# A gated cross-attention and quantised feed-forward block: masks kept as bytes, added as 32-bit words, and a new order of instructions

## What is computed

```
scores = (ctx Wq^T + bq)(ctx Wk^T + bk)^T * H^-0.5 * layernorm(x)
scores = where(attn_mask | padding_mask, -inf, scores)
x = x + tanh(g0) * softmax(scores)
y = layernorm(x)
gate, up = silu(qlinear(y, w_gate)), qlinear(y, w_up)      # I = 2048
x = x + tanh(g1) * qlinear(gate * up, w_down)
```

## Time and profile before

| | |
|---|---|
| median of 3 runs | 228.04 us |
| the profiled execution | 227.88 us |
| its span on the core | 226.1 us |
| TensorE (PE) busy | 201.0 us, 89% |
| VectorE (DVE) busy | 175.3 us, 78% |
| ScalarE (ACT) busy | 131.5 us, 58% |
| GpSimd (POOL) busy | 127.7 us, 56% |

### The profile page before, as it was taken

One profiled execution on the slowest core, in us unless ns is written; L12 is line 12 of the kernel. 1 busy time (PEld: TensorE's weight loads), 2 busy tenths in 40 slices (PEclk: granted clock), 3 DMA queues, 4 the chain that ended last, 5 costly groups with the idle time before them and its releaser, 6 DMA issues.

```text
span 226.1 us, 2874 instructions
## 1 busy us (share of the span) xinstructions
PE 201.0 (89%) x854; PEld 90.8 (40%) x854; DVE 175.3 (78%) x343; ACT 131.5 (58%) x173; POOL 127.7 (56%) x180
## 2 busy tenths in 40 slices
PE   8714526979999998999999999999999999999994
PEld 7201104234444443444444444444444444444441
DVE  0588897899879899699969889897998675786221
ACT  2559986965989410466994305977655525771400
POOL 2898799999999998225168775117994000000000
PEclk9985555799999999999999999999999999999999
DMA  6999979865004466204235632414846626001982
GB/s 222 422 420 417 417 282 372 311 188 226 0 0 93 96 139 117 70 0 96 46 77 108 139 96 72 89 27 94 112 76 117 162 49 139 3 0 20 202 198 93
DMA packets 47360, 32.84 MB, mean 145 GB/s; under 512 B 40944, under 2 KB 41072, under 8 KB 45808
## 3 DMA queue, kind: packets, MB, share of 16 engines
q1 hardware_dynamic: 47200, 32.51, 50.9%
q10 hardware_dynamic: 144, 0.13, 0.3%
HBM read 18.48 MB, written 4.19 MB: 100 GB/s over the span
## 4 chain that ended last, share of the span: by engine, by line
PE 59%; POOL 23%; issue 7%; DVE 4%; DMA 4%; ACT 1%; SPq 0%; POOLq 0%; DVEq 0%
PE pD L978 20%; PE pU L962 19%; PE pG L949 18%; POOL down_w L548 3%; POOL mask_bias L467 2%; POOL up_w L548 2%; PE pA L926 2%; POOL x L504 2%; DMA hid<-in_masks 2%; POOL probs L517 2%; DVE x L1265 2%; POOL gate_w L548 2%; POOL probs L501 2%; DMA xqT<-xq 1%; POOL esd L512 1%
## 5 line engine op out<-in xcount | busy, mean ns | idle before, releaser
L747 ACT ACTIVATE hid<-pG,act_g 128x512 f32<-128x512 f32 x64 | 43.7, 686 | 52.9 <-PE pG L949 52.3
L949 PE MATMUL pG<-gate_w,xqT 128*128 128x512 f16 x256 | 65.0, 387 | 1.7 <-DMA xqT<-xq 1.0
L962 PE MATMUL pU<-up_w,xqT 128*128 128x512 f16 x256 | 62.1, 379 | 1.1 <-DVE up_w L1355 1.1
L978 PE MATMUL pD<-down_w,stage_b 128*128 128x512 f16 x256 | 57.9, 379 | 0.2 <-DMA stage_b<-stage_b 0.2
L1312 DVE TENSOR_TENSOR hid<-pU,hid 128x512 f32<-128x512 f32 x64 | 43.7, 685 | 13.3 <-PE pU L962 11.7
L754 ACT ACTIVATE stage_b<-hid,inv 128x1024 f16<-128x1024 f32 x32 | 35.7, 1141 | 16.1 <-DVE inv L1330 10.4
L949 PEld LDWEIGHTS pG<-gate_w,xqT 128*128 128x128 f16 x256 | 25.2, 99 | 38.0 <-issue 8.9
L962 PEld LDWEIGHTS pU<-up_w,xqT 128*128 128x128 f16 x256 | 24.9, 98 | 31.3 <-DVE up_w L1355 1.2
L978 PEld LDWEIGHTS pD<-down_w,stage_b 128*128 128x128 f16 x256 | 25.0, 98 | 30.6 <-issue 0.6
L555 POOL TENSOR_SCALAR out_scale<-den,act_e,down_k 128x1 f32<-128x1 f32 x16 | 5.4, 339 | 42.2 <-DVE den L1327 42.2
L467 POOL TENSOR_TENSOR mask_bias<-attn_bias,pad_bias 128x512 bf16<-128x512 bf16 x16 | 18.8, 1178 | 8.0 <-DVE mx L1249 7.8
(11 more groups left out here) (86 smaller groups left out, 232.1 us busy)
## 6 DMA issues: line engine op xcount, KB each, us to landing
stage_a<-in_L_ffn_w_gate SPq DMA_DIRECT2D x4, 1024.0 KB, 10.8
stage_b<-in_L_ffn_w_up SPq DMA_DIRECT2D x4, 1024.0 KB, 19.3
stage_a<-in_L_ffn_w_down SPq DMA_DIRECT2D x4, 1024.0 KB, 6.1
stage_b<-in_x SPq DMA_DIRECT2D x2, 1024.0 KB, 6.0
out<-x SPq DMA_DIRECT2D x8, 256.0 KB, 2.5
out<-stage_b SPq DMA_DIRECT2D x8, 256.0 KB, 2.4
ctx_s<-in_ctx SPq DMA_DIRECT2D x4, 256.0 KB, 5.7
x<-in_x SPq DMA_DIRECT2D x2, 512.0 KB, 7.8
```

The lines of the kernel that those rows point to most:

```text
L747: act.activation(hid[:, t % NH, n * 512:(n + 1) * 512], pG[c % NG][:, :], ACT.Silu, scale=act_g[:, t:t + 1]).then_inc(silu_done, 1)
L949: ins = pe.matmul(pG[c % NG][:, :], xqT[:, t // TILES % 2, t % TILES, k, :], gate_w[:, n, k, :], start=k == 0, stop=k == KD - 1)
L962: ins = pe.matmul(pU[c % NU][:, :], xqT[:, t // TILES % 2, t % TILES, k, :], up_w[:, n, k, :], start=k == 0, stop=k == KD - 1)
L978: ins = pe.matmul(pD[t % ND][:, :], hidT[:, t % 2, k, :], down_w[:, k // KD, k % KD, :], start=k == 0, stop=k == KI - 1)
```

## The change

The widenings are gone. The masks stay bytes (0 or 1); GpSimd reads them as 32-bit integers and adds the padding words of a batch to the attention words of all four tiles in one instruction, so a byte becomes 0, 1 or 2. mask_and_max subtracts the bytes from the scores and multiplies by 2^30; scores are scaled by 2^-80 ahead of it, and rstd is scaled back. q, k and ctx get four buffers instead of two, the bytes a buffer of their own.

```diff
-MASKED = -1.5e35
+SMALL = 2.0 ** -80
+BACK = 2.0 ** 30
+V1 = (SMALL * BACK) ** 2
+MASKED = -0.5 * BACK
 NEG = -3.4028234663852886e38
 SCALING = float(H) ** -0.5
...
 bqs = sb("bqs", [P, 1])
-ctx_s = sb("ctx_s", [P, 2, S])
-qT = sb("qT", [P, 2, S])
-kT = sb("kT", [P, 2, S])
-attn_bias = sb("attn_bias", [P, TILES, S], BF16)
-pad_bias = sb("pad_bias", [P, B, S], BF16)
-mask_bias = sb("mask_bias", [P, 2, S], BF16)
+ctx_s = sb("ctx_s", [P, NQ, S])
+qT = sb("qT", [P, NQ, S])
+kT = sb("kT", [P, NQ, S])
+masks_u8 = sb("masks_u8", [P, (TILES + B) * S], U8)
+mask_u8 = sb("mask_u8", [P, 2, TILES * S], U8)
 x01 = sb("x01", [P, 2 * TILES, D])
-probs = sb("probs", [P, TILES, S])
...
 def _(pool):
-    def pad_mask_bias(b0, b1):
-        pool.wait_ge(mask_loaded, 16)
-        pool.tensor_scalar(pad_bias[:, b0:b1, :], pad_u8[:, b0 * S:b1 * S].rearrange("p (b t) -> p b t", t=S),
-                           MASKED, 1.0, ALU.mult, ALU.mult).then_inc(bias_made, 1)
-    def attn_mask_bias(j0, j1):
-        pool.tensor_scalar(attn_bias[:, j0:j1, :], attn_u8[:, j0 * S:j1 * S].rearrange("p (j t) -> p j t", t=S),
-                           MASKED, 1.0, ALU.mult, ALU.mult).then_inc(bias_made, 1)
-    def mask(t):
-        b, j = divmod(t, TILES)
-        pool.wait_ge(bias_made, 2 if t == 0 else 3 if t < TILES else 4)
-        if t >= 2:
-            pool.wait_ge(masked, t - 1)
-        pool.tensor_tensor(mask_bias[:, t % 2, :], attn_bias[:, j, :], pad_bias[:, b, :], ALU.add)\
-            .then_inc(mask_ready, 1)
+    def mask(b):
+        if b == 0:
+            pool.wait_ge(mask_loaded, 16)
+        if b >= 2:
+            pool.wait_ge(masked, TILES * (b - 1))
+        w = S // 4
+        pad = masks_i32[:, (TILES + b) * w:(TILES + b + 1) * w].rearrange("p (j w) -> p j w", j=1)
+        pool.tensor_tensor(mask_i32[b % 2].rearrange("p (j w) -> p j w", w=w),
+                           masks_i32[:, 0:TILES * w].rearrange("p (j w) -> p j w", w=w),
+                           pad.broadcast_to([P, TILES, w]), ALU.add).then_inc(mask_ready, 1)
     def rstd(g):
...
         pool.wait_ge(masked, t1)
-        pool.tensor_scalar(valid[:, t0:t1], mx[:, t0:t1], MASKED / 2, 1.0, ALU.is_gt, ALU.mult)\
+        pool.tensor_scalar(valid[:, t0:t1], mx[:, t0:t1], MASKED, 1.0, ALU.is_gt, ALU.mult)\
             .then_inc(valid_done, 1)
         pool.wait_ge(valid_done, g + 1)
...
         if b == 0:
             act.wait_ge(bqs_done, 1)
-        if b >= 2:
-            act.wait_ge(score_done, TILES * (b - 1))
-        act.activation(qT[:, b % 2, :], pA[:, :], ACT.Identity, scale=SCALING, bias=bqs[:, :])\
+        if b >= NQ:
+            act.wait_ge(score_done, TILES * (b - NQ + 1))
+        act.activation(qT[:, b % NQ, :], pA[:, :], ACT.Identity, scale=SCALING * SMALL, bias=bqs[:, :])\
             .then_inc(q_ready, 1)
...
-        if t >= TILES:
-            quantised_x(dve, t - TILES)
-        dve.scalar_tensor_tensor(probs[:, t % TILES, :], xt(t), mv1[:, t, 0:1], bank[:, :],
+        if t >= NP:
+            quantised_x(dve, t - NP)
+        dve.scalar_tensor_tensor(probs[:, t % NP, :], xt(t), mv1[:, t, 0:1], bank[:, :],
                                  ALU.subtract, ALU.mult).then_inc(scored, 1)
     def mask_and_max(t):
         dve.wait_ge(scored, t + 1)
-        dve.wait_ge(mask_ready, t + 1)
-        dve.tensor_tensor_reduce(probs[:, t % TILES, :], probs[:, t % TILES, :], mask_bias[:, t % 2, :],
-                                 1.0, NEG, ALU.add, ALU.max, mx[:, t:t + 1]).then_inc(masked, 1)
+        b, j = divmod(t, TILES)
+        dve.wait_ge(mask_ready, b + 1)
+        dve.tensor_tensor_reduce(probs[:, t % NP, :], probs[:, t % NP, :], mask_u8[:, b % 2, j * S:(j + 1) * S],
+                                 BACK, NEG, ALU.subtract, ALU.max, mx[:, t:t + 1]).then_inc(masked, 1)
     def gate_sums(g):
```

More of the change, by code:

```diff
@@ L26 @@
 NH = 4
+NQ, NP = 2, 4
 NG, NU, ND = 2, 3, 2
@@ L586, in _ @@
             weight_round(0, 1)
+            weight_round(0, 2)
+            centre(2)
+            std2(1)
+            centre(3)
             gate_scales(0)
-            weight_round(0, 2)
-            std2(1)
-            centre(2)
             weight_round(0, 3)
-            centre(3)
-            mask(6)
             up_scales(0)
             weight_round(1, 0)
+            gate_scales(1)
+            quantise_x(2)
+            up_scales(1)
+            quantise_x(3)
             rstd(2)
             weight_round(1, 1)
-            mask(7)
@@ L599, in _ @@
-            quantise_x(2)
-            gate_scales(1)
-            quantise_x(3)
-            up_scales(1)
             weight_round(1, 2)
-            mask(8)
             weight_round(1, 3)
+            weight_round(2, 0)
             exp_bias(2)
-            weight_round(2, 0)
-            mask(9)
+            mask(3)
             weight_round(2, 1)
             weight_round(2, 2)
+            weight_round(2, 3)
             valid_sums(2)
-            weight_round(2, 3)
+            residual1(4)
@@ L1092, in _ @@
             up(6, 0)
-            gate(7, 0)
+            up(6, 1)
+            down(3, 0)
+            up(6, 2)
+            up(6, 3)
+            down(3, 1)
             down(3, 2)
-            up(6, 1)
             down(3, 3)
@@ L1386, in _ @@
             weight_bound(0, 1)
             stats2(3)
+            weight_bound(0, 2)
+            absmax_x(2)
             stats1(4)
-            weight_bound(0, 2)
+            inverse_std2(1)
             score(4)
-            stats1(5)
+            absmax_x(3)
             mask_and_max(4)
             copy_xT(0)
+            weight_scale(1)
             weight_bound(0, 3)
-            weight_scale(1)
-            inverse_std2(1)
+            reciprocal_scale(0)
+            inverse_x(1)
+            stats1(5)
@@ L1397, in _ @@
             stats1(6)
-            reciprocal_scale(0)
+            weight_bound(1, 0)
             stats1(7)
+            reciprocal_scale(1)
             score(5)
-            weight_bound(1, 0)
+            product(0, 0)
             mask_and_max(5)
-            absmax_x(2)
-            absmax_x(3)
-            product(0, 0)
-            inverse_x(1)
+            copy_xT(1)
+            product(1, 0)
+            weight_scale(2)
+            score(6)
             weight_bound(1, 1)
-            product(1, 0)
@@ L1409, in _ @@
-            score(6)
-            product(0, 1)
             mask_and_max(6)
             score(7)
-            absmax_hidden(0, 0)
-            mask_and_max(7)
-            weight_bound(1, 2)
-            product(1, 1)
-            weight_scale(2)
-            weight_bound(1, 3)
-            product(0, 2)
-            reciprocal_scale(1)
+            weight_bound(1, 2)
+            mask_and_max(7)
+            weight_bound(1, 3)
+            stats1(8)
+            product(0, 1)
+            stats1(9)
@@ L1431, in _ @@
             inverse_hidden(0)
+            product(1, 3)
+            stats1(10)
+            absmax_hidden(1, 1)
+            stats2(4)
+            inverse_hidden(1)
             product(2, 0)
-            absmax_hidden(1, 1)
-            weight_bound(2, 3)
+            stats2(5)
+            absmax_x(4)
             product(2, 1)
-            inverse_hidden(1)
-            absmax_hidden(2, 0)
+            stats1(11)
             product(2, 2)
-            stats2(4)
+            absmax_x(5)
+            stats2(6)
@@ L1440, in _ @@
+            inverse_std2(2)
             product(2, 3)
-            stats2(5)
-            absmax_hidden(2, 1)
-            stats2(6)
-            inverse_hidden(2)
+            inverse_x(2)
+            product(3, 0)
             residual2(0)
+            absmax_x(6)
+            score(8)
+            product(3, 1)
+            mask_and_max(8)
             stats2(7)
-            absmax_x(4)
-            inverse_std2(2)
-            stats1(8)
-            absmax_x(5)
-            product(3, 0)
@@ L1452, in _ @@
-            inverse_x(2)
-            inverse_std2(3)
-            absmax_x(6)
+            product(3, 2)
             residual2(1)
             absmax_x(7)
-            score(8)
-            inverse_x(3)
-            mask_and_max(8)
-            reciprocal_scale(2)
-            product(3, 1)
-            residual2(2)
+            score(9)
+            inverse_std2(3)
+            mask_and_max(9)
+            product(3, 3)
+            reciprocal_scale(2)
+            product(4, 0)
+            inverse_x(3)
```

630 lines of the change are left out of this document (304 added, 326 removed).

## The result

The changed kernel takes 231.53 us (median of 4 runs, 231.44 to 231.78), the kernel before 228.0 beside it (227.93 to 228.21, 4 runs): a ratio of 1.0147, 95% interval 1.0129 to 1.0165. It is 3.5 us slower; 229.7 was forecast, in a range of 225.2 to 232.0. One thing was said wrongly ahead: q, k and ctx keep their two buffers (`NQ, NP = 2, 4` in the kernel).

The account below looks back on a forecast made before the run. Bound by an opening of some 49 us, GpSimd and VectorE preparing TensorE's work, then TensorE's fixed list. List end 223.4 against 222.86 (+0.54) plus 1.3 of stalls gave +1.8 us: 229.7 us, range 225.2 to 232.0.

Parts of the forecast that it names:

- the opening's gain: Before the first weight rounding: 0.95 us won, turned into a loss of 1.8 us by the end of copy_xT(0).
- Mask arithmetic: GpSimd's masks and widenings: four integer adds of 1.25 us replace them, 18 to 19 us less work; byte operand free.
- To the first rounding: Opening: x's second part arrives at 13.4 us, first weight rounding starts near 24.7 us, gain 0.95 us.
- To the first gate: Roundings against VectorE instructions up to copy_xT(0): it ends at 39.1 us, before at 37.33.
- the tie: mask_and_max(4) against rounding 4 near 37 us: copy_xT(0) ends at 38.35 if it wins, 39.9 if it loses.
- of two VectorE instructions in a row the second keeps the way: Opening: a waiting rounding lets two successive VectorE instructions through; read from residual1 and weight_bound in the earlier trace.
- Rival 3: GpSimd gets its turn after every VectorE instruction; copy_xT(0) ends 1.1 us later, 231.6 us in all; chance 0.12.
- From the copy to score(6): copy_xT(0) to score(6): 11.2 us, including 2.2 for mask_and_max(5) against rounding (1, 1); score(6) starts at 50.3.
- The stalls: TensorE waits at up(1, 2) and up(2, 1) for products behind clips: 1.3 us taken, ends 0 and 2.5.
- The work behind: TensorE's list from score(6) on: 173.1 us of work, ending at 223.4 instead of 222.86 before stalls.
- the wait before gate(4, 0): TensorE's old wait of 0.95 us at 88.90 should go, as residual1(4) to quantise_x(4) shortens to about 12 us.
- Rival 1: Roundings and VectorE instructions pass each other; copy_xT(0) ends by 36.2 and the kernel takes 224.6 us; chance 0.27.

Follow-up runs that it names:

- the old order: New mask arithmetic with all five instruction lists in the order of the kernel before, one mask(b) replacing four mask(t), widenings left out: 225.23 us, 0.9874 against the kernel before.

## Why the prediction was right, and where it was off

The sign, the place and the mechanism were right: the opening's gain was lost to VectorE instructions that stand opposite roundings, and waits for products follow behind it. The size was 1.8 us too small, half of what was measured, and it would have been further off had a mask-and-max not got ahead of its rounding by luck (point 4).

1. **Mask arithmetic.** 1.25 us taken for the integer add, 1.27 measured. GpSimd's busy time fell by 19.8 us, 18 to 19 forecast. The two buffers of q, k and ctx change nothing in the sum, since four had been taken at zero. The byte operand costs nothing: an undisturbed mask-and-max takes 0.68 us, the mean is 0.80 (0.823 in the earlier trace rows).
2. **To the first rounding.** x's second part ended the wait as forecast (VectorE's stats start at 13.25, 13.4 forecast), and the rounding started at 24.39 (24.7). The halved clock of the earlier trace rows was misread: its slices stand at half from some 17 us on, not from 23; no term hangs on it. The add opposite residual1(0) costs here, 0.5 us, which the sum had left out; the run with doubled adds and the one with mask(1) in front both show it.
3. **To the first gate.** Forecast copy_xT(0) ended at 39.1, or 39.9 with the tie lost; it lost, at 40.05. But the way there wasn't mine. I had the second residual go straight through and the inverse at 30.5; it came at 31.9. This is the step that failed, "of two VectorE instructions in a row the second keeps the way": true of the earlier trace rows, where the second is a clip with constants, and false for two residuals. Rival 3 had this pair right, and the first clip waiting for rounding 3 (29.79, 1.86 us), with the copy ending at 40.2. Most of the 1.4 us was taken back by luck, at the other side of the same meeting: the roundings, held up by one instruction at a time instead of two, ended at 31.1 instead of 32.3, and the second clip, which I had waiting for the third of them, met nothing. mask_and_max(4) came at 37.47, 0.4 late.
4. **From the copy to score(6).** 11.2 us forecast, 9.25 measured (40.05 to 49.30): mask_and_max(5) came at 47.95, 0.18 us before its rounding, and took 0.68 us. I had counted 2.2 us for it, with the rounding 0.4 us ahead; at a few tenths of a microsecond between them such a meeting can't be called. That is luck too: it made up for 1.5 us of the sum.
5. **The stalls.** The two places named, up(1, 2) and up(2, 1), are the two that waited, but for 3.40 us instead of 1.3 (ends 0 to 2.5). This is the term that was mis-sized most, and it fell outside its own bounds. I had two of three clips meet roundings; all three did (1.83, 1.71 and 2.37 us), the last of them as the third in a row. Taking 1.3 as a middle between 0 and 2.5 assumed that the meetings are independent. They aren't: VectorE is full there, 19.84 of 20 us, so what it loses at one meeting is still owed at the next, and the products stand behind all three.
6. **The work behind.** 173.1 forecast, 173.5 measured, and the wait before gate(4, 0) went.

Sum of the terms: -1.0 (score(6) earlier than forecast), +2.1 (stalls), +0.4 (work) make 1.5 of the 1.8 us; the rest lies around the list.

Rival 1 said that with the copy done by 36.2 the time would be 224.6; the old order had it at 36.3 and took 225.2. That fits its mechanism, though the list is another one; the changed kernel was far from it. Rival 3's number, 231.6, hit; its rule only half, as the mask-and-max behind a clip didn't wait. The Trainium skill (SBUF — State Buffer, "SBUF: two separate sides") has whichever engine starts first keep the shared ports for the whole instruction. The standstills shown fit that, a rounding of 1.97 us or an add of 1.27 waited out in full. Read as a turn for each side, it is right for residual to residual (4.31 us) and clip to residual (2.37), and wrong for residual to clip (0.68) and clip to mask-and-max (0.68 at 52.88).

## What to carry to other kernels

- Work taken off one engine is worth what its neighbours can do with it. Here 2.8 us came from the arithmetic and 6.3 were given back by the order, in part at least because it put residuals, clips and mask-and-max instructions of VectorE opposite GpSimd's long ones. Time a change in the arithmetic in the old order first.
- Where an engine is full, add up what stands still on it in front of the step that the next engine needs, and carry each loss on to it, instead of pricing each wait by itself. The busy time of the same count of instructions (175.3 to 182.8 us; 174.8 in the old order) shows the loss at once.
- Of the VectorE instructions that a rounding stops (residuals, clips, mask-and-max), between two roundings one gets through if the next takes its scalar from SBUF; with constants two do, and no trace shows three. The float32 statistics and reductions, with one input, were never stopped (absmax_x at 29.19 took 0.67 us during a rounding), nor were the products, which read one input from PSUM (0.67 to 0.70 us in all traces), and they are what to put opposite a rounding.
